# A deformable-convolution pair: the third stage's ScalarE and TensorE programs as loops, and a new order at the hand-over from the second stage

## The chip, the cores and the metric

The kernel runs on one core of one Trainium2 chip. The metric is the device time of the whole program in microseconds (us); the time before is the median of three runs.

## The reference

```python
h = _bn_lrelu(_dcnv2(x, w_off1, b_off1, w1, b1, 1, 0), g1, bb1, m1, v1)   # x: 8 x 512 x 52 x 52
h = _bn_lrelu(_dcnv2(h, w_off2, b_off2, w2, b2, 3, 1), g2, bb2, m2, v2)   # h: 256 channels in, 512 out
return x + h

def _dcnv2(x, w_off, b_off, w, b, k, pad):
    om = conv(x, w_off) + b_off            # per pixel and tap: dy, dx, mask
    oy, ox, mask = om[:, :P], om[:, P:2*P], sigmoid(om[:, 2*P:])
    val = bilinear(x, base_y + oy, base_x + ox) * mask      # P = k*k samples per pixel
    return einsum('ncphw,ocp->nohw', val, w) + b
```

`_bn_lrelu` is a batch norm followed by a leaky ReLU of slope 0.1. All arithmetic is float32.

## The kernel before

The 8 x 52 x 52 pixels are 169 tiles of 128 pixels (`TILES`), in 13 chunks of 13 tiles. Three stages follow each other, and every engine runs its part of all three in program order.

**First stage.** A 1x1 convolution: x is loaded by SP, multiplied by TensorE, and its 256 channels per pixel are written to a table in DRAM. TensorE's and ScalarE's parts are hardware loops (`Fori`) over chunks (L390, L461).

**Second stage.** One gather per tile (GpSimd, L702) fetches the four neighbours of each sampled pixel; ScalarE and VectorE weigh and add them (`near` L780, `add_far` L877, `add_upper` L893, `add_lower` L901, `activate` L910). The result h goes to a second DRAM table (`table_writes`, L302, on ScalarE's queue) and, transposed by TensorE (L715) and copied by ScalarE (L788), into a 3x3 convolution that gives the offsets of the third stage: `convolve` (TensorE, L730) per band of 8 image rows, `fold_band` (ScalarE, L802), `turn` (TensorE, L748). From the offsets a chunk's plan (weights and row indices) is made by `modulation` and `hats` (ScalarE, L815 to L832) and by `place` and `modulate` (VectorE, L926 to L945); SP writes it to DRAM (L676) and loads it again four tiles at a time (L295).

**Third stage.** 42 blocks ("supers") of 4, 3 or 2 tiles, nine taps each. A unit is one tap of one tile: a gather of 128 x 1024 floats (GpSimd, L1181) into one of 18 slots, then `scale_near` (ScalarE, L1195), `add_far` (VectorE, L1246), `scale_line` (ScalarE, L1203), `add_line` (VectorE, L1254). Four units make a tap: TensorE transposes it (L1314, 8 matmuls), ScalarE and VectorE split it into a high and a low part (`upper` L1209, `lower` L1261), and `multiply` (L1327) does 24 matmuls of 128 x 512. TensorE does the transposes of tap r and then the multiply of tap r-1. After nine taps the sums are evacuated (L1218) and finished (L1268, L1278).

**The hand-over.** The third stage's first eight units (`BEGUN`) are already scaled and added at the end of the second stage. ScalarE's loop runs on for `DRAIN = 14` steps after the last tile and does in each what of copies, folds and begun units falls due. TensorE does the first transposes in that drain, but the first multiply only after `pe.wait_ge(gate_ready, CHUNKS)`: its first matmuls would write PSUM bank 0, from which ScalarE and VectorE still read the last offsets. VectorE does the last chunk's `place` and `modulate` after the eight units, and ScalarE its `hats`, before both go on with tap 2. GpSimd's gathers are in program order; gathers 8 to 17 go to slots that the second stage still uses, first those in `h_other`, then in `h_stage` (free once the table's last writes have landed), then in the transposed h (`IN_H_T`, free after the last `convolve`) and in the offset sums (`IN_Q`, free after the last `turn`).

The helper that writes third-stage programs has two forms, both there before: `in_full` writes all taps out, `position` writes the first and last ones out and puts the middle in a loop of 19 rounds, 18 taps (two blocks) a round. Before, only `in_full` is used.

## Time and profile before

| | us |
|---|---|
| three runs | 3228.51, 3241.77, 3260.52 |
| median | 3241.77 |
| the profiled execution | 3246.28 |
| its span from the first to the last instruction | 3244.3 |
| mean granted TensorE clock | 0.984 of full speed |

The profile and all its rows are of the one profiled execution, 4.5 us above the median. 2.0 us of it lie outside the span.

### The profile page before, as it was taken

Reading aid. Unit: us, or ns where it says so; the run is one execution under the profiler, and the core shown is the slowest. Engines: PE = TensorE matmul, PEld = TensorE weight load, DVE = VectorE, ACT = ScalarE, POOL = GpSimd, SP = SyncE. Lnnn points to the kernel's source line nnn. Section 1 sums busy time; section 2 is a strip of 40 time slices with the busy share of each in tenths; the row PEclk is TensorE's granted clock in tenths of the full one; section 3 lists DMA queues with packets and bytes.
Section 4 is the critical chain, followed back from the end, with each engine's and each line's share of the span. In section 5 each row is a group of like instructions: output and inputs, shape, how many; then the busy total and the mean of one; then the engine's idle time right before and its main releaser. Section 6 shows DMA issues by size and latency. Waiting matters only on the chain.

```text
span 3244.3 us, 48817 instructions
## 1 busy us (share of the span) xinstructions
PE 3042.3 (94%) x15660; PEld 2474.0 (76%) x15660; DVE 2741.7 (85%) x4746; ACT 2498.5 (77%) x4658; POOL 1744.9 (54%) x1708
## 2 busy tenths in 40 slices
PE   8997888889999999999999999999999999999999
PEld 7996455478777778777878777778777777777879
DVE  5557999879888889888989888889888888888987
ACT  5665777778787878788888787878788778778876
POOL 0003444456666566665666666666665656665652
PEclk9998999989999999999999999999999999999999
DMA  9998999999999999998999999999999999998995
GB/s 324 366 353 318 387 347 332 321 377 355 356 361 345 364 356 347 351 369 323 372 367 353 354 370 339 370 353 343 358 357 333 360 343 330 345 360 324 356 346 188
DMA packets 431464, 1125.10 MB, mean 347 GB/s; under 512 B 42956, under 2 KB 171468, under 8 KB 431232
## 3 DMA queue, kind: packets, MB, share of 16 engines
q0 software_dynamic: 244784, 891.09, 74.2%
q1 hardware_dynamic: 118608, 163.05, 14.1%
q10 hardware_dynamic: 67840, 68.16, 6.1%
q8 instruction: 110, 1.80, 0.2%
q14 instruction: 122, 1.00, 0.1%
HBM read 1002.15 MB, written 137.04 MB: 351 GB/s over the span
## 4 chain that ended last, share of the span: by engine, by line
PE 44%; DVE 32%; ACT 12%; issue 8%; another core or an unknown queue 3%; ACTq 1%; DMA 0%; SPq 0%; DVEq 0%; POOLq 0%
PE psum_t L1327 29%; DVE arena L1246 11%; DVE val_lo L1261 6%; PE psum_t L400 5%; PE psum_t L1314 5%; ACT psum_t L1195 5%; PE psum_t L730 4%; DVE arena L1254 4%; ACT arena L1203 2%; DVE val_first L1254 2%; DVE z_sb L1268 2%; ACT val_hi L1209 2%; DVE arena L877 2%; DVE arena L1278 1%
## 5 line engine op out<-in xcount | busy, mean ns | idle before, releaser
L1181 POOL DMA_INDIRECT arena<-table,plan_in x1521 | 1571.4, 1033 | 1017.6 <-DVE arena L1254 444.4
L1327 PE MATMUL psum_t<-val_hi,w_hi 128*128 128x512 f32 (+2 forms) x3096 | 1247.2, 403 | 50.9 <-ACT z_sb L1218 30.8
L1327 PE MATMUL psum_t<-val_hi,w_lo 128*128 128x512 f32 (+2 forms) x3096 | 1205.7, 389 | 8.9 <-issue 8.7
L1327 PE MATMUL psum_t<-val_lo,w_hi 128*128 128x512 f32 (+2 forms) x3096 | 1204.0, 389 | 4.5 <-issue 4.3
L1195 ACT ACTIVATE psum_t<-arena,plan_in 128x512 f32<-128x512 f32 x1521 | 1042.4, 685 | 211.6 <-DVE arena L1246 119.9
L1246 DVE SCALAR_TENSOR_TENSOR arena<-arena,plan_in,psum_t 128x512 f32<-128x512 f32 x1521 | 1129.3, 742 | 72.4 <-issue 38.6
L1327 PEld LDWEIGHTS psum_t<-val_hi,w_hi 128*128 128x128 f32 x3096 | 587.7, 190 | 187.8 <-ACT z_sb L1218 50.4
L1261 DVE TENSOR_TENSOR val_lo<-psum_t,val_hi 128x1024 fp32r<-128x1024 f32 (+2 forms) x387 | 465.5, 1203 | 275.3 <-ACT val_hi L1209 167.5
L1327 PEld LDWEIGHTS psum_t<-val_hi,w_lo 128*128 128x128 f32 x3096 | 586.0, 189 | 132.8 <-issue 11.8
L1327 PEld LDWEIGHTS psum_t<-val_lo,w_hi 128*128 128x128 f32 x3096 | 588.9, 190 | 108.1 <-issue 5.9
L1209 ACT ACTIVATE val_hi<-psum_t 128x1024 fp32r<-128x1024 f32 (+2 forms) x387 | 386.4, 998 | 272.7 <-remote 185.5
L1203 ACT ACTIVATE arena<-arena,plan_in 128x256 f32<-128x256 f32 x1014 | 503.5, 497 | 0.1
L1254 DVE SCALAR_TENSOR_TENSOR arena<-arena,plan_in 128x256 f32<-128x256 f32 x1014 | 487.8, 481 | 0.0
L1314 PE MATMUL psum_t<-ident,arena 128*128 128x128 f32 x2028 | 271.3, 277 | 54.1 <-DVE arena L1254 45.1
L1314 PEld LDWEIGHTS psum_t<-ident,arena 128*128 128x128 f32 x2028 | 237.6, 143 | 99.1 <-DVE arena L1254 63.8
L702 POOL DMA_INDIRECT arena<-table,arena x169 | 164.2, 972 | 259.6 <-DVE arena L901 109.5
L1203 ACT ACTIVATE val_first<-arena,plan_in 128x256 f32<-128x256 f32 x507 | 253.2, 499 | 0.1
L1254 DVE SCALAR_TENSOR_TENSOR val_first<-arena,plan_in,val_first 128x256 f32<-128x256 f32 x507 | 243.3, 480 | 0.0
L730 PE MATMUL psum_t<-arena 128*96 128x408 f32 (+1 forms) x624 | 237.1, 517 | 0.0
L400 PE MATMUL psum_t<-w_hi,val_hi 128*128 128x260 f32 x676 | 197.8, 293 | 28.5 <-DVE val_lo L520 27.8
L520 DVE TENSOR_TENSOR val_lo<-arena,val_hi 128x512 fp32r<-128x512 f32 x169 | 116.3, 691 | 123.9 <-ACT val_hi L418 123.4
L400 PE MATMUL psum_t<-w_hi,val_lo 128*128 128x260 f32 x676 | 193.0, 286 | 0.0
(90 smaller groups left out, 2396.8 us busy)
## 6 DMA issues: line engine op xcount, KB each, us to landing
arena<-x SPq DMA_DIRECT2D x90, 512.0 KB, 4.7
table<-arena ACTq DMA_DIRECT2D x40, 896.0 KB, 7.3
out<-arena SPq DMA_DIRECT2D x136, 256.0 KB
table<-arena ACTq DMA_DIRECT2D x40, 768.0 KB, 7.1
arena<-x SPq DMA_DIRECT2D x70, 384.0 KB, 6.3
arena<-table,plan_in POOLq DMA_INDIRECT x1521
table<-table SPq DMA_DIRECT2D x32, 512.0 KB
arena<-w POOLq DMA_DIRECT2D x9, 512.0 KB, 6.5
```

The costliest lines, as they stand in the source:

```text
L400: last = nc.tensor.matmul(y_bank(j), a[:, X_SLOT[j], k, :], b[:, k, :], start=(k == 0 and a is x_hi and b is w1_hi), stop=(k == KT1 - 1 an ...
L702: nc.gpsimd.indirect_dma_start(gather1[:, t % SLOTS, :], None, table1[0:image_end(t) + WIDTH, :], bass.IndirectOffsetOnAxis(ap=index1[:, t ...
L730: last = nc.tensor.matmul(out_rows[:, :, to:to + w], woff_sb[:, kt, dx, :], h_rows[:, :, at:at + w], start=(nth == 0 and kt == 0), stop=(n ...
L1181: nc.gpsimd.indirect_dma_start(landing(r, i)[:, :], None, rows, bass.IndirectOffsetOnAxis(ap=row.bitcast(u32), axis=0))\
L1195: nc.scalar.activation(psum_near[:, unit(r, i) % NEARS, :], landing(r, i)[:, 0:2 * C_MID], ACT.Identity, scale=weight(r, i, 0)).then_inc(n ...
L1203: nc.scalar.activation(val(r, i), landing(r, i)[:, 0:C_MID], ACT.Identity, scale=weight(r, i, 2)).then_inc(line_scaled, 1)
L1209: nc.scalar.activation(val_hi[:, r % 2, :, 0:n], psum_val[:, :, 0:n], ACT.Identity).then_inc(hi_ready, 1)
L1246: nc.vector.scalar_tensor_tensor(out=landing(r, i)[:, 0:2 * C_MID], in0=landing(r, i)[:, 2 * C_MID:4 * C_MID], scalar=weight(r, i, 1), in1 ...
L1254: nc.vector.scalar_tensor_tensor(out=v, in0=landing(r, i)[:, C_MID:2 * C_MID], scalar=weight(r, i, 3), in1=v, op0=ALU.mult, op1=ALU.add).t ...
L1261: nc.vector.tensor_tensor(val_lo[:, r % 2, :, 0:n], psum_val[:, :, 0:n], val_hi[:, r % 2, :, 0:n].bitcast(f32), ALU.subtract)\
L1314: last = nc.tensor.transpose(psum_val[:, kt, i * P:(i + 1) * P], val(r, i)[:, kt * P:(kt + 1) * P], ident[:, :])
L1327: last = nc.tensor.matmul(psum_acc[:, oc, 0:n], a[:, w, oc * P:(oc + 1) * P], b[:, r % 2, kt, 0:n], start=(w == 0 and a is w2_hi and b is ...
```

## The change

- **Third stage.** ScalarE and TensorE use `position` (a loop of 19 rounds, its bound `ROUNDS` and its 18 taken back edges the same on both); VectorE stays written out. In the built program TensorE's loop body is 622 instructions of which 576 are matmuls, and each matmul stands for a weight load and a multiply in the trace: 1198 together. ScalarE's body is 299 instructions. Waits on semaphores in the loop compare with a register that is computed ahead of them.
- **Hand-over, TensorE.** Convolutions are done one or two steps after the pair of tiles that completes a band, turns one step earlier. The first multiply goes ahead of the wait for the offsets: it does output blocks 3, 1, 2 and only before block 0 waits. Its transposes are followed by those of taps 1 and 2.
- **Hand-over, ScalarE and VectorE.** ScalarE's drain is an explicit list. VectorE's `place` is cut in two: `place_first` (the read of PSUM) stays at the hand-over, `place_rest` goes to tap 7 of the third stage, `hats` of the last chunk to tap 8 and `modulate` to tap 9.
- **Hand-over, GpSimd.** The slots' order is `h_other`, `h_t`, the offset sums, and `h_stage` last.
- **Stores.** The second table is written by SP, not by ScalarE's queue, with the last part of the last chunk cut in two; a chunk's plan is stored after the next chunk's table.

```diff
+LATE_TILE = 10
+PLACE_REST_AT = 7
...
-        PLACE = [(TILES + n) % SLOTS for n in range(SLOTS)] + IN_H_OTHER + IN_H_STAGE + IN_H_T + IN_Q
+        PLACE = [(TILES + n) % SLOTS for n in range(SLOTS)] + IN_H_OTHER + IN_H_T + IN_Q + IN_H_STAGE
...
-            DRAIN = 14
-            PLACED = 9
+            DRAIN = 9
+            FOLDED = 6
+            PLACED = 8
...
             def on_sync(sp):
-                for c in range(CHUNKS):
+                def store_h(c):
+                    for half in range(2):
+                        for j, tiles in parts_of(c, half):
+                            sp.wait_ge(h_ready, c * CHUNK + j + tiles)
+                            table_writes(sp, table2, h_buf(c), c, (j, tiles), table2_written[c % 2][half], copies_of(c))
...
+                for c in range(CHUNKS):
+                    store_h(c)
+                    if c:
+                        store_plan(c - 1)
...
+                store_plan(CHUNKS - 1)
...
-                    if t == last_tile(BAND_COUNT - 1) + PLACED:
+                    for band, nth in CONVOLVE_AT.get(t, ()):
+                        convolve(band, nth)
+                    if t == TILES + 2:
                         begin_transpose()
-                    for nth in range(3):
-                        if t - 3 - nth in BAND_AT:
-                            convolve(BAND_AT[t - 3 - nth], nth)
...
-                pe.wait_ge(chain2, (CHUNKS - 1) * (CHAIN + 1) + 1)
-                pe.wait_ge(gate_ready, CHUNKS)
+                def offsets_read():
+                    pe.wait_ge(chain2, (CHUNKS - 1) * (CHAIN + 1) + 1)
+                    pe.wait_ge(gate_ready, CHUNKS)
+
+                begin_multiply(offsets_read)
...
+                    act.wait_ge(lines_ready, TILES - 1)
+                    begin_unit(0)
+                    fold_band(before_last, 1)
+                    copy_h_t(last_pair - 1)
+                    fold_band(before_last, 2)
+                    act.wait_ge(lines_ready, TILES)
+                    act.wait_ge(upper_added, TILES)
+                    begin_unit(1)
+                    copy_h_t(last_pair)
+                    for u in range(2, 6):
+                        begin_unit(u)
+                    for dy in range(3):
+                        fold_band(last_but_one, dy)
                     begin_upper()
+                    for dy in range(3):
+                        fold_band(last, dy)
+                    for u in range(6, BEGUN):
+                        begin_unit(u)
                     modulation(CHUNKS - 1)
-                    hats(CHUNKS - 1)
+                    return lambda: hats(CHUNKS - 1)
...
-                def step(it, r):
+                def step(it, r, late_place, late_modulate):
+                    if r == PLACE_REST_AT:
+                        late_place()
+                    if r == PLACE_REST_AT + 2:
+                        late_modulate()
...
-                return lambda: transpose(0, 0), lambda: in_full(step, after=1, first=1)
+                def begin_multiply(offsets_read):
+                    multiply(0, 0, order=(3, 1, 2, 0), first_free=offsets_read)
+                    transpose(0, 1)
+
+                return lambda: transpose(0, 0), begin_multiply, lambda: position(pe, step, after=1, first=2)
```

In ScalarE's third stage `in_full(step, after=5, first=2)` becomes `position(act, ..., after=5, first=2)`.

TensorE at the hand-over, from the last bands to the first multiply. L715, L730, L748, L1314 and L1327 are the transposes of h, `convolve`, `turn`, and the third stage's transposes and multiply. Before:

```order
L715 MATMUL psum_t<-ident,arena 128x128 x2
L730 MATMUL psum_t<-arena 96x416 x2
L748 MATMUL psum_t<-arena 128x27 x3
L730 MATMUL psum_t<-arena 96x8x51 x4
L730 MATMUL psum_t<-arena 96x416 x2
L748 MATMUL psum_t<-arena 128x27 x4
L730 MATMUL psum_t<-arena 96x8x51 x4
L748 MATMUL psum_t<-arena 128x27 x3
L1314 MATMUL psum_t<-ident,val_first 128x128 x8
L748 MATMUL psum_t<-arena 128x27 x4
L1314 MATMUL psum_t<-ident,arena 128x128 x8
L1327 MATMUL psum_t<-val_hi,w_hi 128x512
```

Now (the same five are L744, L759, L777, L1374 and L1389):

```order
L744 MATMUL psum_t<-ident,arena 128x128 x2
L759 MATMUL psum_t<-arena 96x416 x2
L759 MATMUL psum_t<-arena 96x8x51 x4
L777 MATMUL psum_t<-arena 128x27 x4
L1374 MATMUL psum_t<-ident,val_first 128x128 x8
L777 MATMUL psum_t<-arena 128x27 x7
L1389 MATMUL psum_t<-val_hi,w_hi 128x512
```

After the last pair of h only three convolution groups are left, the first third-stage transposes stand ahead of the last seven turn matmuls, and the first multiply follows those turns with no transposes between.

VectorE at the same place. L1246, L1254 and L1261 are `add_far`, `add_line` and `lower`; L926 to L935 are `place`, L945 is `modulate`. Before, from the fifth unit's `add_line` on:

```order
L1254 SCALAR_TENSOR_TENSOR arena<-arena,plan_in 128x256
L1261 TENSOR_TENSOR val_lo<-psum_t,val_hi 128x1024
L926 TENSOR_TENSOR arena<-psum_t,arena 128x252
L929 TENSOR_SCALAR arena<-arena 128x252
L930 TENSOR_SCALAR arena<-arena 128x252
L931 TENSOR_TENSOR arena<-arena 128x252
L932 SCALAR_TENSOR_TENSOR arena<-arena 128x14x9
L935 TENSOR_TENSOR plan_sb<-arena 128x14x9
L945 TENSOR_TENSOR plan_sb<-arena 128x14x9 x2
L1246 SCALAR_TENSOR_TENSOR arena<-arena,plan_in,psum_t 128x512
```

Now, from the sixth unit's `add_far` on (L1294, L1302, L1309, L989 and L963 are `add_far`, `add_line`, `lower`, `modulate` and `place_first`):

```order
L1294 SCALAR_TENSOR_TENSOR arena<-arena,plan_in,psum_t 128x512
L1302 SCALAR_TENSOR_TENSOR val_first<-arena,plan_in,val_first 128x256
L989 TENSOR_TENSOR plan_sb<-arena 128x13x9 x2
L1309 TENSOR_TENSOR val_lo<-psum_t,val_hi 128x1024
L1294 SCALAR_TENSOR_TENSOR arena<-arena,plan_in,psum_t 128x512
L1302 SCALAR_TENSOR_TENSOR arena<-arena,plan_in 128x256
L1294 SCALAR_TENSOR_TENSOR arena<-arena,plan_in,psum_t 128x512
L963 TENSOR_TENSOR arena<-psum_t,arena 128x252
L1294 SCALAR_TENSOR_TENSOR arena<-arena,plan_in,psum_t 128x512
```

`lower` of tap 0 stands after six units instead of eight, and one plan instruction is left of eight before the ninth unit's `add_far`.

## Rows read from the trace of the kernel before

**Rows 1.** The page: busy time of each engine, and the chain's shares by engine.
```profile
PE 3042.3 (94%) x15660; PEld 2474.0 (76%) x15660; DVE 2741.7 (85%) x4746; ACT 2498.5 (77%) x4658; POOL 1744.9 (54%) x1708
PE 44%; DVE 32%; ACT 12%; issue 8%; another core or an unknown queue 3%; ACTq 1%; DMA 0%; SPq 0%; DVEq 0%; POOLq 0%
```
**Rows 2.** Windows: PE, PEld, DVE, ACT, POOL busy us; PEclk, DMA share, GB/s.
```profile
626.00:640.00 14.00, 11.85 (x50) 6.83 (x48) 6.09 (x12) 10.88 (x22) 3.75 (x4) 1.00 0.82 277
640.00:654.00 14.00, 4.04 (x23) 3.94 (x24) 11.12 (x23) 11.07 (x24) 9.97 (x11) 0.58 0.78 253
...
1300.00:3200.00 1900.00, 1818.59 (x8984) 1499.14 (x8984) 1657.83 (x2764) 1518.42 (x2635) 1156.51 (x1118) 0.99 0.95 351
```
**Rows 3.** The chain in order of time, start of the third stage: start us, us, what.
```profile
684.35 0.87 PE psum_t L1314 x8
685.22 5.46 PE psum_t L1327 x24
```
**Rows 4.** Timeline, TensorE at the hand-over: start us, us, what, idle before.
```profile
641.25 1.09 PE L1314 MATMUL psum_t<-ident,val_first 128*128 128x128 f32 x8 [3.40 <-DVE val_first L1254]
...
652.56 1.94 PE L1314 MATMUL psum_t<-ident,arena 128*128 128x128 f32 x8 [8.71 <-issue]
654.15 0.78 PE L1327 MATMUL psum_t<-val_hi,w_hi 128*128 128x512 f32 x1
...
661.34 0.48 PE L1327 MATMUL psum_t<-val_hi,w_hi 128*128 128x512 f32 x1
```
**Rows 5.** Timeline, ScalarE and VectorE at the hand-over.
```profile
625.95 0.46 DVE L945 TENSOR_TENSOR plan_sb<-arena 128x117 f32<-128x117 f32 x2
...
643.44 1.23 DVE L1261 TENSOR_TENSOR val_lo<-psum_t,val_hi 128x1024 fp32r<-128x1024 f32 x1 [0.60 <-ACT val_hi L1209]
...
649.05 0.75 DVE L1246 SCALAR_TENSOR_TENSOR arena<-arena,plan_in,psum_t 128x512 f32<-128x512 f32 x1
...
650.11 0.74 DVE L1246 SCALAR_TENSOR_TENSOR arena<-arena,plan_in,psum_t 128x512 f32<-128x512 f32 x1
...
624.34 0.39 ACT L832 ACTIVATE arena<-arena 128x117 f32<-128x117 f32 x1
...
642.38 1.02 ACT L1209 ACTIVATE val_hi<-psum_t 128x1024 fp32r<-128x1024 f32 x1 [0.18 <-PE psum_t L1314]
...
648.35 0.67 ACT L1195 ACTIVATE psum_t<-arena,plan_in 128x512 f32<-128x512 f32 x1
...
649.36 0.67 ACT L1195 ACTIVATE psum_t<-arena,plan_in 128x512 f32<-128x512 f32 x1
```
**Rows 6.** Timeline, GpSimd's gathers of the third stage's units 10 and 11.
```profile
630.09 0.94 POOL L1181 DMA_INDIRECT arena<-table,plan_in  x1 [0.30 <-issue]
640.98 1.03 POOL L1181 DMA_INDIRECT arena<-table,plan_in  x1 [9.95 <-issue]
```
**Rows 7.** Waits of VectorE, 700 to 3200 us, and (last) 330 to 612 us.
```profile
DVE val_lo L1261 <- ACT val_hi L1209: 144.7, 68, 6.6
DVE val_lo L1261 <- issue: 106.3, 70, 3.5
...
DVE arena L877 <- ACT psum_t L780: 9.7, 13, 4.0
```
**Rows 8.** The first stage's loop branches, TensorE and ScalarE: duration ns min/median/max.
```profile
L390 PEldq COMPARE_BRANCH  x13: 76/208/235, 35.2 to 287.0; - x13
...
L461 ACTq COMPARE_BRANCH  x10: 40/45/58, 53.9 to 234.6; - x10
```
**Rows 9.** DMA queues that carry instructions: 36 to 290 us (first), 700 to 3200 us.
```profile
q14 instruction: 5, 0.04, 0.0%
...
q8 instruction: 94, 1.54, 0.2%
q14 instruction: 98, 0.80, 0.1%
```
**Rows 10.** DMA issues from the table's line L302: issue to landing.
```profile
DMA to landing us min/median/max: 3.9/7.1/10.3
```

More of the change, by code:

```diff
@@ L287, in copies_of, with parts_of, written_to @@
             return 2 if c < WHOLE_CHUNKS else 1
-        def written_to(b, chunks):
-            return sum(copies_of(c) * 16 for c in range(b, chunks, 2))
+        def parts_of(c, half):
+            j, n = HALVES[half]
+            if c == CHUNKS - 1 and half == 1:
+                return (j, LATE_TILE - j), (LATE_TILE, j + n - LATE_TILE)
+            return ((j, n),)
+        def written_to(b, half, chunks):
+            return sum(copies_of(c) * len(parts_of(c, half)) * 16 for c in range(b, chunks, 2))
         def load_plan(sp, s):
@@ L644, in second_stage, with complete_at @@
             BAND_AT = {last_tile(band): band for band in range(BAND_COUNT)}
+            def complete_at(band):
+                return next(t for t in range(last_tile(band), TILES) if t in PAIR_AT)
+            CONVOLVE_AT = {}
+            for band in range(BAND_COUNT):
+                for nth, after in enumerate((1, 1, 2)):
+                    CONVOLVE_AT.setdefault(complete_at(band) + after, []).append((band, nth))
             def band_pieces(band, dy):
@@ L1239, in step, with go_on @@
                             evacuate(it, ended, EVACUATE[r % TAPS][i])
-                return begin_unit, lambda: upper(0, 0), lambda: in_full(step, after=5, first=2)
+                def go_on(late_hats):
+                    position(act, lambda it, r: step(it, r, late_hats), after=5, first=2)
+                return begin_unit, lambda: upper(0, 0), go_on
             def on_vector(dve):
@@ L1316, in transpose, with multiply @@
                     last.then_inc(transposed, 1)
-                def multiply(it, r):
+                def multiply(it, r, order=range(KT1), first_free=None):
                     n, k = tiles_of(r) * P, r % TAPS
                     pe.wait_ge(lo_ready, taps_to(it, r))
-                    for oc in range(KT1):
+                    for oc in order:
+                        if oc == 0 and first_free:
+                            first_free()
                         if k == 0 and exists(it, r - 1):
```

109 lines of the change are left out of this document (56 added, 53 removed).

## The prediction

> **What bounds the kernel now.** I read the page first for the engines' shares and the chain [rows 1]. TensorE is busy for 94% of the span and the chain goes through it for 44%, through VectorE for 32%; ScalarE has 12% of it, GpSimd and the DMA queues next to nothing. The windows then say where it isn't so [rows 2]: from 1300 to 3200 us TensorE is busy for 1819 of 1900 us, and DMA moves 351 GB/s at a share of 0.95, so memory is close behind; but from 640 to 654 us TensorE is busy for 4.0 of 14 us, at a granted clock of 0.58, so over four fifths of that stretch were at 1.2 GHz. That is the hand-over. In the steady third stage a tap costs 5.5 us of multiply and 0.87 us of transposes, 6.37 us [rows 3]; the 387 taps are 2465 us of it, and nothing in this change touches that. So the change can act in two places: the hand-over, once, and whatever the loops add or save at each round.
>
> **The hand-over.** The reader is to see four moments of TensorE [rows 4]: the first transposes at 641.25 us after an idle 3.4 (the last turns follow at once), then, after 8.7 us of nothing, tap 1's transposes at 652.56, the first multiply at 654.15, and the second multiply at 661.34, from which it is in step with the other engines. What it waited for is VectorE: its last work of the second stage is at 625.95, and the ninth unit's `add_far` only at 649.05 [rows 5], 23 us for eight units, a `lower` and a plan. I rebuild the new order from 624.7 us, the end of ScalarE's last `hats` before (624.34 + 0.39) [rows 5]. A unit takes ScalarE 1.01 us (from 648.35 to 649.36) and VectorE 1.06 (649.05 to 650.11) [rows 5]; `upper` takes 1.02 and `lower` 1.23 [rows 5]. Folds, smaller than a near's 0.67, I put at 0.4, an estimate.
> - ScalarE: first near 0.6, fold, copy and fold 1.6 (the copy waits for a pair that VectorE ends near 625.2), second near 0.6, short copy 0.3, units 2 to 5 in 4.1: 631.9. VectorE follows by 0.6 and ends tap 0 at 632.5.
> - TensorE: transposes 632.5 to 633.4. ScalarE is in three folds till 633.1, then `upper` till 634.4, VectorE's `lower` till 635.7. The last folds end at 635.9, the seven turns at 637.1.
> - First multiply 637.1 to 642.6 at 5.5 us, transposes of tap 1 till 643.5, then `upper`, `lower`, tap 2's transposes (3.1 us, in which TensorE idles for 2.2): second multiply at 646.6. Block 0 of the first multiply needs `modulation` and `place_first`, near 639: it is last in the list and doesn't wait.
>
> 661.3 - 646.6 = 14.7 us. Against it: TensorE's clock was at half after it had idled [rows 2], and it will idle here around 630 to 636 too; 24 matmuls at half clock cost up to 5.5 us more, so I take half of that. **Term 1: -12 us**, between -17 and -5.
>
> The gathers must keep up. Unit 11 was issued only at 640.98, after 10.9 us without an issue [rows 6], since its slot in `h_stage` waited for the table's last write. Now unit 11 takes the slot that the last `convolve` frees, units 12 and 13 those behind the turns (637), and only unit 14 needs the table. Gathers go out every 1.25 us, and units are used every 1.0 to 1.6, so I price this at nothing; if it does bind, the gain goes with it (rival B).
>
> `place_rest`, `hats` and `modulate` of the last chunk (five, six and two short instructions, some 2 us on each of two engines) go to taps 7 to 9. VectorE idles there: before `lower` it waited 144.7 + 106.3 us in 387 taps, 0.65 us a tap [rows 7]. Spread over three taps that covers most. SP stores the last plan only then, and x's first residual block and the third block's plan queue behind it on SP; both are used four taps or 25 us later. **Term 2: +1 us**, 0 to +4.
>
> **The second stage.** Moving the table's stores from ScalarE's queue to SP and the earlier convolve, fold and turn change nothing that ends there: VectorE ends that stage and waited for ScalarE for 9.7 us in 282 [rows 7]. Behind SP's new waits stand the plan's stores and the first two plan loads, which have chunks of time; VectorE's reuse of an h buffer waits for these stores two chunks later. TensorE may now stop for `copy_h_t` a step earlier, and behind it is the next transpose; it has room. **Term 3: -2 us**, 0 to -8.
>
> **The loops.** 18 back edges on each of two engines. The nearest rows are the first stage's: a taken branch of TensorE takes 0.208 us, one of ScalarE 0.045 [rows 8]. Register work for waits is computed while the engine still has queued work. At 0.2 us an edge: **term 4: +4 us**. That is the lower bound, and it holds only if the first instructions of the body are still on the engine when it branches. The first stage shows that for short bodies: from 36 to 290 us, over twelve of TensorE's back edges, no packet came on queue 8 and five on queue 14 [rows 9], while in straight code queue 8 brought 94 packets for some 24,000 of TensorE's instructions, so about 256 each. That body is 340 instructions, more than a packet. The new one is 1198, nearly five packets; ScalarE's is 299 against a first-stage body of 88, with smaller packets (0.80 MB in 98) of half the size. No row shows bodies this long. Upper bound: a fetch at each edge, rival A.
>
> The Trainium skill ("Runtime: NRT & Kernel Launch", section on instruction fetch mechanics) speaks against this change: a taken branch to a target outside the current window of two pages must wait for the page to be fetched. The same section gives TensorE room for 2048 instructions and the others 512, by which both bodies would stay. By the first sentence the result is rival A's, by the second mine; the trace's long first-stage loop without a fetch agrees with either.
>
> **Sum.** -12 + 1 - 2 + 4 = -9 us. The profiled execution would go from 3246.3 to 3237; it stood 4.5 above the median, so the median goes from 3241.8 to **3232 us** (3232.8, rounded down).
>
> **Rivals.**
> - **A, each back edge fetches (slower).** Place: ScalarE before tap 0 of each round. Price: the shortest landing of a DMA in these rows is 3.9 us [rows 10]; less the 0.65 us that VectorE idles in a tap, 3.2 us reach TensorE; TensorE's own fetch runs at the same time and is covered in part by queued matmuls. 18 x 3.2 = 58 instead of 4: 3232 + 54 = 3286. With the median landing of 7.1, 18 x 6.4 = 116: 3344. It decides from 1.8 us an edge on (32 us, 1% over the median before, is reached at (32 + 13) / 18 = 2.5). For it: nothing shows such a body kept. Against: the 340-instruction loop spans two packets and was kept. Chance 0.27; about 0.2 of it is over 1% slower.
> - **B, the gain at the hand-over is eaten.** Gathers, half clock or a late turn leave the second multiply at 659 or so: 3232 + 12 = 3244. For it: DMA is at 0.82 and 0.78 in these windows [rows 2], and TensorE at half clock. Chance 0.15.
> - **C, more than I sum up.** If both bodies stay, the code packets of [rows 9] vanish, 0.3% of DMA time or 8 us: 3224, or 3217 with the best of term 1. Chance 0.1. Faster by over 1% needs 32 us, and I find no stretch that holds them.
> - My forecast, 3232: 0.48.
>
> A tenth of a per cent can't be told here: the three runs spread over 32 us, 1%, and 1% is what a measurement of this kernel can tell from no change. The range takes in C's 3217 with some room for the median of a few runs, 3212, and above reaches A's first price: 3212 to 3286. Left out are A's dearer half and stray runs, under 0.2. Faster by over 1%: 0.05 (C and a low median). Slower by over 1%: 0.2. Within 1%: 0.75.
>
> **What would show it.** Term 1: the second multiply within 21 us of VectorE's last second-stage instruction (before 35 us), and unit 11's gather by 635. Term 2: no gap of VectorE over 2 us at taps 7 to 9 and none at the first residual. Term 4 against A: idle time of ScalarE and TensorE once in 18 taps, at the branch's line, and packets on queues 8 and 14; in my case almost no instruction packets from 700 to 3100 us on queue 8. The forecast is wrong if fetches at the edges cost more than 2.5 us each, or if the plan's late store starves the gathers of the third block.

## The result, and the profile after

The kernel after takes 3285.8 us, the median of 4 runs (3278.87 to 3295.32), against 3247.1 us of the kernel before beside it (4 runs, 3228.51 to 3260.52): ratio 1.0128, 95% interval 1.0106 to 1.015. It is slower by 1.3%, where 3232 and "no difference" had been forecast; 3285.8 lies just inside the forecast range, whose top was the price of rival A. Its profiled execution took 3295.3 us (span 3293.4), 9.5 above its median; that of before 3246.3. So 49.1 us lie between the two spans, and 38.7 between the medians.

The page after, the engines' busy time and the chain by engine; they answer to [rows 1]:

```profile
span 3293.4 us, 49916 instructions
## 1 busy us (share of the span) xinstructions
PE 3063.6 (93%) x15660; PEld 2485.3 (75%) x15660; DVE 2741.9 (83%) x4746; ACT 2493.1 (76%) x4658; POOL 1745.1 (53%) x1708
...
## 4 chain that ended last, share of the span: by engine, by line
DVE 40%; PE 26%; issue 14%; ACT 13%; another core or an unknown queue 5%; ACTq 1%; DMA 1%; SPq 0%; DVEq 0%; POOL 0%; POOLq 0%
```

TensorE's share of the chain fell from 44% to 26% and VectorE's rose from 32% to 40%. TensorE waits more; who makes it wait is the question. Windows after, the same as in [rows 2] (us; busy time of PE, PEld, DVE, ACT, POOL; granted clock, DMA share, GB/s):

```profile
626.00:640.00 14.00, 13.13 (x57) 7.24 (x55) 12.08 (x28) 11.82 (x25) 7.20 (x8) 1.00 0.99 357
640.00:654.00 14.00, 11.46 (x54) 8.26 (x53) 10.37 (x19) 12.97 (x27) 5.62 (x7) 0.88 0.80 289
1300.00:3200.00 1900.00, 1800.27 (x8809) 1478.37 (x8807) 1632.88 (x2721) 1490.63 (x2592) 1140.97 (x1101) 0.98 0.94 345
```

The hand-over looks as meant: from 640 to 654 us TensorE is busy for 11.5 us in place of 4.0. The steady third stage is worse: 1800.3 us of 1900 in place of 1818.6. Packets of instructions from 700 to 3200 us, and the branches of the loop (L1086; duration ns min/median/max), which answer to [rows 9] and [rows 8]:

```profile
q14 instruction: 60, 0.49, 0.1%
q8 instruction: 10, 0.16, 0.0%
...
L1086 ACTq COMPARE_BRANCH  x19: 40/45/50, 892.6 to 3126.9; - x19
...
L1086 PEldq COMPARE_BRANCH  x19: 83/215/217, 909.0 to 3139.4; - x19
```

TensorE's queue 8 brings 10 packets where it brought 94, ScalarE's sequencer goes on 0.2 us after each branch, TensorE's 0.06: both bodies stay on their engines. Rival A's fetch doesn't happen. VectorE's last instruction of the second stage and TensorE at the hand-over, which answer to [rows 4, 5]:

```profile
637.64 0.43 DVE L948 SCALAR_TENSOR_TENSOR arena<-arena 128x256 f32<-128x256 f32 x1
...
645.65 1.07 PE L1374 MATMUL psum_t<-ident,val_first 128*128 128x128 f32 x8
646.56 0.75 PE L777 MATMUL psum_t<-arena 97*128 97x27 f32 x6
649.38 1.07 PE L777 MATMUL psum_t<-arena 97*128 97x27 f32 x8 [2.07 <-ACT arena L833]
650.30 0.47 PE L1389 MATMUL psum_t<-val_hi,w_hi 128*128 128x512 f32 x1
...
657.47 1.03 PE L1374 MATMUL psum_t<-ident,arena 128*128 128x128 f32 x8
668.88 1.97 PE L1374 MATMUL psum_t<-ident,arena 128*128 128x128 f32 x8 [10.37 <-issue]
670.50 0.78 PE L1389 MATMUL psum_t<-val_hi,w_hi 128*128 128x512 f32 x1
```

The first transposes stand 8.0 us behind VectorE's last instruction of the second stage (15.3 before) and the first multiply 12.7 (28.2 before). But that last instruction (the first row) is itself at 637.64 us, not at 625.95 [rows 5]: **the second stage ends 11.7 us later** (from the last `activate` of the one, at 625.61, to that of the other it is 12.0). And tap 2's transposes, then, come only after 10.4 idle us.

All runs below are read by four stretches of their one profiled execution, from the starts of VectorE's `add_upper` (one per tile) and of TensorE's transposes (a tap's first weight load) in each timeline: tiles 13 to 156 of the second stage; tile 156 to the third stage's first transposes; those to tap 18's; and the 342 taps from there to tap 360, 19 rounds. (387 taps of nine a block are 43 blocks: 41 of four tiles, one of three, one of two.)

### The profile page after: what moved, and what is told of

The parts are those of the page before. It is cut to its first block, busy times and chain, and to the rows that moved or that the text cites. A ratio compares the mean times of both kernels' runs of the same rounds, so it can differ in the third digit from the quotient of the medians.

```text
span 3293.4 us, 49916 instructions
## 1 busy us (share of the span) xinstructions
PE 3063.6 (93%) x15660; PEld 2485.3 (75%) x15660; DVE 2741.9 (83%) x4746; ACT 2493.1 (76%) x4658; POOL 1745.1 (53%) x1708
## 4 chain that ended last, share of the span: by engine, by line
DVE 40%; PE 26%; issue 14%; ACT 13%; another core or an unknown queue 5%; ACTq 1%; DMA 1%; SPq 0%; DVEq 0%; POOL 0%; POOLq 0%
DVE arena L1294 16%; PE psum_t L1389 15%; DVE val_lo L1309 8%; DVE arena L1302 6%; PE psum_t L408 5%; PE psum_t L759 3%; ACT psum_t L1238 3%; DVE val_first L1302 3%; ACT arena L1246 3%; PE psum_t L1374 3%; DVE z_sb L1316 3%; DVE arena L1326 2%; ACT val_hi L1252 1%; ACT psum_t L811 1%
## 5 line engine op out<-in xcount | busy, mean ns | idle before, releaser
L1389 PE MATMUL psum_t<-val_hi,w_hi 128*128 128x512 f32 (+2 forms) x3096 | 1251.4, 404 | 44.0 <-issue 24.2
L1389 PE MATMUL psum_t<-val_lo,w_hi 128*128 128x512 f32 (+2 forms) x3096 | 1210.1, 391 | 5.8 <-issue 5.5
L1389 PE MATMUL psum_t<-val_hi,w_lo 128*128 128x512 f32 (+2 forms) x3096 | 1209.1, 391 | 5.5 <-issue 5.3
L1294 DVE SCALAR_TENSOR_TENSOR arena<-arena,plan_in,psum_t 128x512 f32<-128x512 f32 x1521 | 1124.5, 739 | 52.4 <-ACT psum_t L1238 37.8
L1309 DVE TENSOR_TENSOR val_lo<-psum_t,val_hi 128x1024 fp32r<-128x1024 f32 (+2 forms) x387 | 464.5, 1200 | 334.3 <-ACT val_hi L1252 180.9
L1389 PEld LDWEIGHTS psum_t<-val_hi,w_hi 128*128 128x128 f32 x3096 | 591.0, 191 | 176.7 <-issue 38.8
L1389 PEld LDWEIGHTS psum_t<-val_hi,w_lo 128*128 128x128 f32 x3096 | 589.6, 190 | 131.2 <-issue 9.0
L1389 PEld LDWEIGHTS psum_t<-val_lo,w_hi 128*128 128x128 f32 x3096 | 591.5, 191 | 111.9 <-issue 8.8
L1246 ACT ACTIVATE arena<-arena,plan_in 128x256 f32<-128x256 f32 x1014 | 503.1, 496 | 0.0
L1302 DVE SCALAR_TENSOR_TENSOR arena<-arena,plan_in 128x256 f32<-128x256 f32 x1014 | 484.3, 478 | 0.0
L1374 PE MATMUL psum_t<-ident,arena 128*128 128x128 f32 x2028 | 273.6, 279 | 84.0 <-DVE arena L1302 73.3
L1374 PEld LDWEIGHTS psum_t<-ident,arena 128*128 128x128 f32 x2028 | 237.9, 143 | 131.8 <-issue 99.8
L759 PE MATMUL psum_t<-arena 128*96 128x408 f32 (+1 forms) x624 | 243.3, 528 | 39.5 <-ACT arena L819 25.4
L1246 ACT ACTIVATE val_first<-arena,plan_in 128x256 f32<-128x256 f32 x507 | 253.0, 499 | 0.0
L1302 DVE SCALAR_TENSOR_TENSOR val_first<-arena,plan_in,val_first 128x256 f32<-128x256 f32 x507 | 242.1, 477 | 0.0
L759 PEld LDWEIGHTS psum_t<-arena 128*96 128x96 f32 x624 | 97.5, 167 | 136.3 <-issue 80.9
```

What stands on the lines that cost most here:

```text
L759: last = nc.tensor.matmul(out_rows[:, :, to:to + w], woff_sb[:, kt, dx, :], h_rows[:, :, at:at + w], start=(nth == 0 and kt == 0), stop=(n ...
L1246: nc.scalar.activation(val(r, i), landing(r, i)[:, 0:C_MID], ACT.Identity, scale=weight(r, i, 2)).then_inc(line_scaled, 1)
L1294: nc.vector.scalar_tensor_tensor(out=landing(r, i)[:, 0:2 * C_MID], in0=landing(r, i)[:, 2 * C_MID:4 * C_MID], scalar=weight(r, i, 1), in1 ...
L1302: nc.vector.scalar_tensor_tensor(out=v, in0=landing(r, i)[:, C_MID:2 * C_MID], scalar=weight(r, i, 3), in1=v, op0=ALU.mult, op1=ALU.add).t ...
L1309: nc.vector.tensor_tensor(val_lo[:, r % 2, :, 0:n], psum_val[:, :, 0:n], val_hi[:, r % 2, :, 0:n].bitcast(f32), ALU.subtract)\
L1374: last = nc.tensor.transpose(psum_val[:, kt, i * P:(i + 1) * P], val(r, i)[:, kt * P:(kt + 1) * P], ident[:, :])
```

## The experiments

Each run's ratio is to executions of the kernel before beside it, on the same chip. The runs stand in five groups, and the kernel before alone takes two clearly different times in them: 3227.3, 3253.6 and 3249.0 us in runs 1 to 4, 9 to 12, 17 and 18 (the slow chip; the result's 3247.1 is of this kind), and 3075.3 and 3074.8 us in runs 5 to 8 and 13 to 16 (the quick chip). The two names are short for these times; whether it is the chip that differs isn't shown: the record gives the number 0 to the chip of runs 5 to 8, quick, and to that of runs 9 to 12, slow. What the traces show to differ is in the last section. `Old drain` means that the hand-over and the plan steps are those of the kernel before, too; `new` has the new ones.

| run | loops | second stage | chip | ratio (95%) | tiles 13-156 | to transposes | taps 0-18 | 19 rounds |
|---|---|---|---|---|---|---|---|---|
| before | none | old | slow | 1 | 288.2 | 40.6 | 131.9 | 2323.9 |
| after | both | new | slow | 1.0128 (1.0106-1.0150) | 297.5 | 33.6 | 141.5 | 2356.2 |
| e9, after again | both | new | slow | 1.0130 (1.0104-1.0156) | 297.3 | 33.7 | 143.1 | 2360.5 |
| e1 | none | new | slow | 1.0050 (1.0033-1.0068) | 297.9 | 33.6 | 139.9 | 2301.1 |
| e12 | TensorE | new | slow | 1.0064 (1.0042-1.0086) | 297.8 | 33.6 | 140.9 | 2337.9 |
| e17 | ScalarE | new | slow | 1.0040 (1.0017-1.0062) | 297.1 | 33.6 | 140.2 | 2322.2 |
| e3 | both | old, old drain | slow | 1.0093 (1.0073-1.0113) | 284.7 | 40.6 | 135.7 | 2327.3 |
| e10, as e3 | both | old, old drain | slow | 1.0077 (1.0057-1.0097) | 291.4 | 40.5 | 134.9 | 2356.4 |
| e4 | none | convolutions new, rest old, old drain | slow | 1.0165 (1.0146-1.0183) | 333.6 | 43.1 | 132.8 | 2307.1 |
| e2 | both | convolutions old, rest new | slow | 1.0446 (1.0425-1.0466) | 390.7 | 41.1 | 137.8 | 2340.7 |
| e11 | none | old, new drain | slow | 1.0002 (0.9985-1.0020) | 286.0 | 37.7 | 140.5 | 2327.8 |
| e18 | none | old, new drain | slow | 0.9990 (0.9969-1.0011) | 282.4 | 35.5 | 141.1 | 2323.6 |
| e14, after again | both | new | quick | 1.0004 (0.9995-1.0013) | 293.8 | 33.6 | 121.0 | 2170.6 |
| e16, as e1 | none | new | quick | 1.0005 (0.9996-1.0014) | 294.3 | 33.6 | 121.6 | 2170.6 |
| e5 | TensorE | new | quick | 1.0003 (0.9994-1.0012) | 292.0 | 33.6 | 120.5 | 2170.6 |
| e6, e13 | ScalarE | new | quick | 1.0001, 1.0000 (both ±0.0009) | 293.8, 292.2 | 33.7, 33.6 | 120.8, 120.7 | 2170.6 |
| e15, as e3 | both | old, old drain | quick | 1.0001 (0.9992-1.0010) | 285.9 | 40.5 | 120.6 | 2170.6 |
| e8 | both, shifted | old, old drain | quick | 1.0047 (1.0034-1.0061) | 286.3 | 40.5 | 120.5 | 2184.7 |
| e7, as e11 | none | old, new drain | quick | 0.9975 (0.9966-0.9985) | 282.5 | 36.0 | 120.6 | 2170.6 |

**First group: loops and second stage, each undone and each alone.** e1 writes both third stages out:

```diff
-                    position(act, lambda it, r: step(it, r, late_hats), after=5, first=2)
+                    in_full(lambda it, r: step(it, r, late_hats), after=5, first=2)
...
-                return lambda: transpose(0, 0), begin_multiply, lambda: position(pe, step, after=1, first=2)
+                return lambda: transpose(0, 0), begin_multiply, lambda: in_full(step, after=1, first=2)
```

> The changed kernel with the loops of the third stage on ScalarE and TensorE undone: both engines are written out in full again, everything else as after. Theory L (the loops cost about 1.5 us a round beyond what their branches take, seen as 122.3 against 124.0 us for a round of 18 taps): about 27 us less than the kernel after, 3259 us, and tap times at the last two taps of a round back at 6.7 and 6.3 us. Rival R (the loops cost nothing, the rounds run longer because of what the hand-over or the plan steps left behind): 3284 to 3286 us. Both expect VectorE to end the second stage at 638 us as in the kernel after.

3241.4 us, ratio 1.0050. The kernel before took 3227.3 beside it, so the ratios are to be compared: from 1.0128 and 1.0130 it is 0.0079 less, 26 us, as theory L said (27). The two kernels did not run beside each other, and each ratio is known to about 0.002. VectorE still ends the second stage as late as in the kernel after. e3 is the other way round, the kernel before with `in_full` changed to `position` for ScalarE and TensorE:

> The kernel before with nothing changed but the third stage of ScalarE and TensorE as loops over pairs of blocks. Theory L: 3247 + 27 = 3274 us. Rival R: 3247 to 3251 us (18 back edges at about 0.2 us).

1.0093, and 1.0077 when repeated (e10): 30 and 25 us, each beside the kernel before. The pairs agree: on the slow chip both loops cost 25 to 30 us, 1.4 to 1.7 us for each of 18 back edges, and rival R is out. e2 and e4 were to do the same for the convolutions' places, e2 with this line in the kernel after, e4 with the new table of places in the kernel before:

```diff
-                    CONVOLVE_AT.setdefault(complete_at(band) + after, []).append((band, nth))
+                    at = complete_at(band) + after if band >= BAND_COUNT - 4 else last_tile(band) + 3 + nth
+                    CONVOLVE_AT.setdefault(at, []).append((band, nth))
```

> The changed kernel with the convolutions of all but the last four bands back at their old places on TensorE, one step (4 matmuls) in each of the tiles last+3, +4 and +5, in place of two steps at the tile right after the last transposes and one behind them. Folds, turns, stores on SP, loops as after. Theory S (the early convolutions wait for ScalarE's copies with the next transposes queued behind them, so the copy of the next pair and the near scaling behind it come late, about 1 us a chunk): VectorE ends the second stage near 627 us in place of 638, and the whole takes 10 to 12 us less, 3275 us. Rival Q (the second stage is slower because SP issues its stores, or because the folds and the tail come a tile earlier): second stage still ends at 636 to 638, 3284 to 3286 us.

> The kernel before with nothing changed but the places of the convolutions on TensorE: those of the kernel after, with folds one tile later than there and turns where they were. Theory S: second stage of VectorE ends near 637 us in place of 626, whole 3257 to 3259 us. Rival Q: 3247 us.

Both theories missed: 1.0446 (3375.4 us) and 1.0165 (3279.9). Moving the convolutions without the folds breaks the step between the two engines. Waits of e2 from 345 to 600 us (us in total, times, longest; L834 is the fold, L760 the convolution, L745 the transposes of h, L812 `near`, L916 `add_far`):

```profile
ACT arena L834 <- PE psum_t L760: 106.3, 29, 6.5
...
PE psum_t L745 <- DVE arena L949: 59.6, 28, 3.7
...
DVE arena L916 <- ACT psum_t L812: 68.4, 25, 5.2
```

ScalarE stands in front of each fold until TensorE has convolved, `near` stands behind the fold, and VectorE behind `near`. The engines stand in a ring: VectorE ends a pair of tiles, TensorE transposes and convolves it, ScalarE copies, folds and scales the next tile, and VectorE goes on with that. These two runs show how dear a broken step in that ring is, not what the change costs in it; for that, all places had to go back together.

**Second group, on the quick chip.** e5 undoes ScalarE's loop alone, e6 TensorE's (one of the two lines above each). e7 undoes both and puts convolutions, folds, turns and the tail's copy of all but the last chunk back where the kernel before has them:

```diff
+                    at = complete_at(band) + after if band >= BAND_COUNT - 4 else last_tile(band) + 3 + nth
...
+                        if t == last_tile(band) + (8 if band >= BAND_COUNT - 4 else 9):
+                            turn(band)
...
+                                if t == last_tile(band) + (6 if band >= BAND_COUNT - 4 else 7) + dy:
+                                    fold_band(band, dy)
...
-                            if j == 8:
+                            if j == (9 if c < CHUNKS - 1 else 8):
                                 keep_tail(c - 1)
```

> The changed kernel with ScalarE's third stage written out again and TensorE's left as a loop. The loops together cost 29 us (the kernel before with both loops took 1.0093 of before). Theory A (ScalarE's loop is what makes the last-but-one tap of a round late, since ScalarE is at its back edge about 3 us ahead of that tap's transposes): this run is within 5 us of the changed kernel with both written out, a ratio of 1.005. Theory T (TensorE's loop costs it): a ratio of 1.013 to 1.014, as the changed kernel.

> The changed kernel with TensorE's third stage written out again and ScalarE's left as a loop. Theory A: ratio 1.013 to 1.014. Theory T: 1.005. If each engine's loop costs a part, the two runs add up: their ratios less 1.005 sum to about 0.009.

> The changed kernel with both loops undone and with convolutions, folds, turns and the tail's copy of all but the last chunk at the places of the kernel before (convolve at last+3, +4, +5, fold at +7 to +9, turn at +9, tail at tile 9), so that only the stores on SP, the drain of the last chunk and the moved plan steps are new. Theory S (the early convolutions and folds as a whole cost the second stage 11 us): VectorE ends the second stage at 626 to 628 us in place of 638, the ratio falls from 1.005 to 1.000 to 1.002. Rival Q (the stores on SP cost it): the second stage still ends at 636 to 638 us, ratio 1.005. If the new drain gains what was forecast, 12 us, and nothing takes it back, 0.996 to 0.998.

e5 and e6 came out the same, 1.0003 and 1.0001, and say nothing of A and T, since here no version's loops could be told from none (e14 and e15 below). e7 is the one that matters: 3067.3 us, 0.9975, 8.0 us under the kernel before, and by the ratios 9 us under e16, which differs from it only in the old places. VectorE's tiles 13 to 156 take 282.5 us in place of 294.3. So **theory S in its wide form holds**: the new places of convolve, fold, turn and tail cost it, not the stores on SP (rival Q), which e7 keeps. How is seen in the waits from 345 to 600 us, of e16 (new places; L759 convolution, L819 copy of h, L833 fold, L811 `near`, L915 `add_far`):

```profile
PE psum_t L759 <- ACT arena L819: 20.0, 20, 1.6
PE psum_t L759 <- ACT arena L833: 10.4, 10, 1.3
...
ACT arena L819 <- issue: 53.3, 29, 2.9
ACT arena L819 <- PE psum_t L744: 5.9, 10, 1.8
...
DVE arena L915 <- ACT psum_t L811: 11.7, 17, 1.0
```

and of e7 (old places; L745 transposes of h, L760 convolution, L835 fold, L821 copy, L813 `near`, L918 `add_far`):

```profile
PE psum_t L745 <- DVE arena L951: 28.1, 20, 3.3
...
ACT arena L835 <- PE psum_t L760: 36.4, 40, 1.7
ACT arena L821 <- issue: 14.7, 29, 1.3
...
DVE arena L918 <- ACT psum_t L813: 3.2, 10, 1.1
```

With the old places TensorE waits for VectorE alone, for new tiles. With the new ones it stands in front of a convolution until ScalarE has copied the pair (20 times, 20.0 us) or folded (10.4), and the next pair's transposes stand behind the convolution. ScalarE then waits for those transposes in front of its next copy, 53.3 us in place of 14.7, the next `near` stands behind the copy, and VectorE waits 11.7 us in place of 3.2. (The profile calls most of this wait `issue`; that it is one for the transposes is read from `copy_h_t`, which waits for their mark, and from the 5.9 us that are put down to L744.) In all ScalarE idles here little more than with the old places, 59 us against 51; of those 51, 36.4 stand in front of the folds, now all stand in front of the copies. So the rows show where the idle time moved to and that VectorE's grew; the links between are read from the program. Which of the moved places does it was not separated; e2 and e4 show that they can't be moved one by one.

e8 starts a loop's body four taps later, in the kernel before with both loops:

```diff
-                for r in range(first, ROUND_TAPS):
+                for r in range(first, ROUND_TAPS + 4):
...
-                    for r in range(ROUND_TAPS):
+                    for r in range(4, ROUND_TAPS + 4):
```

> The kernel before with both loops of the third stage, but with a loop's body starting four taps later (tap 4 of a pair of blocks, where no wait of TensorE was seen), so that the back edges fall elsewhere in the ring of waits; the same 18 or 19 back edges. Theory edge (each back edge costs about 1.5 us wherever it stands): 1.009. Theory place (it costs because it falls on the taps where the block changes and TensorE's transposes are late anyway): 1.002 or less.

1.0047, and e15 without the shift 1.0001: 14 us, 0.8 at each back edge. But neither theory is right. After the shift ScalarE's sequencer stands still for 5.1 us behind every taken branch (5.04 to 5.23, once 4.88) where it stood 0.2. Packets of instructions from 900 to 3000 us, e8 and then e15, and ScalarE behind the branch at 1226.60 of e8:

```profile
q14 instruction: 136, 1.11, 0.1%
...
q14 instruction: 51, 0.42, 0.1%
...
1229.86 0.52 ACT L1203 ACTIVATE val_first<-arena,plan_in 128x256 f32<-128x256 f32 x1
1231.96 0.69 ACT L1195 ACTIVATE psum_t<-arena,plan_in 128x512 f32<-128x512 f32 x1 [1.58 <-DVE arena L1246]
```

85 more packets, 4.7 for each of the 18 back edges. ScalarE has 3.7 us of work queued and then idles 1.6 us in front of `near`. This is rival A after all, in another kernel: a body of 301 instructions that begins elsewhere in the code is fetched at each round, one of 299 was not. The edit changed both the body's length and its start, and no run separates them.

**Third group, on the slow chip again.**

> The changed kernel itself, unchanged, beside the three below on one chip; runs 5 to 8 came from a chip on which the kernel before takes 3075 us and the third stage's rounds take 114.2 us with TensorE never idle, runs 1 to 4 from one with 3227 us and rounds of 121 to 124 us. If this is the quick chip: theory C (a back edge costs only when both engines have one, since the shifted pair of loops cost 14 us there and a single loop nothing) gives 1.003 to 1.005; theory N (unshifted loops are free where TensorE never waits) gives 1.000. If the slow chip: 1.013 again.

> The kernel before with both loops. Quick chip: theory C 1.003 to 1.005, with the taps after a back edge at 6.5 to 6.7 us in place of 6.33; theory N 1.000. Slow chip: 1.009 again.

> The changed kernel without loops and with the old places of convolutions, folds, turns and tail for all but the last chunk. Quick chip: 0.9975 again. Slow chip: theory S says that the 11 us of the second stage come back there too (the ratio of both loops undone was 1.005), 1.001 or less, with VectorE ending the second stage near 626 us.

> The changed kernel with only TensorE's loop kept. Quick chip: 1.0003 again. Slow chip: theory A (ScalarE's back edge is the one that delays) 1.005; theory T (TensorE's) 1.013; both in part, between.

e9 and e10 repeat 1.013 and 1.008. e11, 1.0002, repeats theory S on the slow chip: 0.0048 less than e1's ratio, 16 us, of which 11.9 are in tiles 13 to 156. e12, 1.0064, excludes theory T, TensorE's loop as the whole cost.

**Fourth group, on the quick chip.**

> The changed kernel with only ScalarE's loop kept. Slow chip: if ScalarE's loop carries the 27 us, 1.012 to 1.013; if the cost needs both, 1.005 to 1.007. Quick chip: 1.000 again.

> The changed kernel itself. Slow chip 1.013 again. Quick chip: 1.000 if loops are free there (one loop alone gave 1.000), 1.003 to 1.005 if two loops cost what the shifted pair cost.

> The kernel before with both loops, not shifted. The trace of the shifted pair showed ScalarE's sequencer standing 5.1 us behind every back edge where the unshifted ones stand 0.2 us, so on the quick chip 1.000 to 1.001 is expected here and 1.0047 was the price of those 5.1 us. Slow chip 1.008 again.

> The changed kernel with both loops undone. Quick chip: the same as with one loop, 1.000, which makes the new order of the second stage worth plus 8 us there against the run with the old order (0.9975). Slow chip: 1.005 again.

All four lie within 0.05% of the kernel before. Here the change as a whole does nothing, and the loops cost nothing: 19 rounds take 2170.6 us in every kernel but e8, 6.35 us a tap. Windows of the kernel after from 1300 to 3000 us, slow chip, then quick chip:

```profile
1300.00:3000.00 1700.00, 1605.20 (x7851) 1317.22 (x7850) 1457.55 (x2428) 1330.75 (x2315) 1016.29 (x981) 0.98 0.94 345
...
1300.00:3000.00 1700.00, 1700.00 (x8575) 1429.24 (x8574) 1587.58 (x2644) 1452.27 (x2526) 1114.35 (x1071) 1.00 0.99 375
```

**Fifth group, slow chip.** e17 is e6 again. e18 is e11 with the switch to the new places one band later and the tail's copy at its old place in the last chunk too, since VectorE had taken 28.1 us (e7: 26.3) for its last twelve tiles, where the kernel after took 24.2 and that before 23.4.

> The changed kernel with only ScalarE's loop kept. Slow chip: if ScalarE's loop carries the 27 us, 1.012 to 1.013; if the cost needs both engines' loops, 1.005 to 1.007. Quick chip: 1.000 for the third time.

> The changed kernel with both loops undone, and with the old places of convolutions, folds and turns kept up to the last chunk's first band (the earlier run switched one band sooner, and VectorE then took 26.3 us for the last twelve tiles in place of 23.4 to 24.2), the tail's copy at its old place throughout. New: the drain, the stores on SP, the moved plan steps. If the switch is smoother now, 2 to 3 us below the earlier run: 0.9965 on the quick chip, 0.999 on the slow one. If the pile-up only moves, 0.9975 and 1.000.

e17, 1.0040, excludes theory A too. Neither loop alone can be told from none (1.0064 and 1.0040 against 1.0050, each known to about 0.002), together they cost 0.0079: on this chip it takes both, or nearly so (ratios from three groups of runs are compared here). e18 is at 0.9990 on the slow chip, within its interval of 1 and of e11; the last twelve tiles took 25.7 us. The best shown version is e7, 0.25% under the kernel before on the quick chip and, as e11, even with it on the slow one.

## Why the prediction was wrong, step by step

**Term 1, hand-over, -12 (-17 to -5).** The mechanism was right. Behind VectorE's last second-stage instruction the first transposes were forecast at 6.5 us and came at 8.0, the first multiply at 11.2 and came at 12.7 (before 15.3 and 28.2). The second multiply was forecast at 20.7 us; on the quick chip it came at 26.5 and in the result at 32.9, before 35.4. TensorE and ScalarE there, e14, VectorE's last instruction at 634.11:

```profile
646.76 0.47 PE L1389 MATMUL psum_t<-val_hi,w_hi 128*128 128x512 f32 x1
...
653.93 1.03 PE L1374 MATMUL psum_t<-ident,arena 128*128 128x128 f32 x8
659.02 1.97 PE L1374 MATMUL psum_t<-ident,arena 128*128 128x128 f32 x8 [4.05 <-DVE arena L1302]
660.64 0.77 PE L1389 MATMUL psum_t<-val_hi,w_hi 128*128 128x512 f32 x1
...
654.63 0.69 ACT L1238 ACTIVATE psum_t<-arena,plan_in 128x512 f32<-128x512 f32 x1 [1.35 <-DMA arena<-table,plan_in]
```

Of the missing 5.8 us, 1.5 are the late start, 1.7 the first multiply, which runs at 1.2 GHz in part, 1.9 the wait for tap 2, of which 1.35 is ScalarE's wait for a gather (the gathers, of which the prediction said "I price this at nothing"), and 0.75 tap 2's transposes at half clock. The second multiply began at half clock too. Unit 11's gather kept its forecast (8.2 us behind VectorE's last instruction in the kernel after, forecast 9), but unit 12's then waited 4.5 us for the last turns and went out 13.6 us behind it, where 11 had been assumed. At tap 18 the gain measured from tile 156 is 161.1 - 154.6 = 6.5 us on the quick chip: half the term, inside its range. On the slow chip the first transposes gain the same 7.0, and at tap 18 nothing is left: taps 0 to 18 take 137.8 to 143.1 us with the new drain against 131.9 to 135.7 with the old one (121 against 120.6 on the quick chip). Of the 9.6 us between the kernels after and before, 3.8 lie in the step from tap 1's transposes to tap 2's (11.6 us for 7.8), where TensorE idles for the 10.4 us of the row at 668.88 above, and 3.4 in that from tap 9's to tap 10's (term 2). At the first of them ScalarE's split of tap 1 came 7 us behind the end of its transposes (657.47 + 1.03):

```profile
665.49 1.02 ACT L1252 ACTIVATE val_hi<-psum_t 128x1024 fp32r<-128x1024 f32 x1 [6.32 <-remote]
```

That is rival B's outcome, though its reasons, half clock and gathers, explain only what the quick chip shows; on the slow one it is late splits of the kind described in the last section, whose cause is open.

**Term 2, moved plan steps, +1.** On the quick chip taps 9 to 18 take 57.1 us, nine times 6.35, so nothing was lost there. On the slow one the step from tap 9's transposes to tap 10's takes 8.8 to 9.8 us in all eight runs with the moved steps, and 6.2 to 7.6 in the four without (before, e3, e4, e10); VectorE waits there up to 6.0 us behind ScalarE's `val_hi`. Some 2 to 3 us more than forecast may so belong to this term, but the same runs also have the new drain, and none has one without the other: it stays open.

**Term 3, second stage, -2: this step failed first.** Its sentence "TensorE may now stop for `copy_h_t` a step earlier, and behind it is the next transpose; it has room" named the mechanism and took the room for granted. TensorE's waits for VectorE with the old places (28.1 us in e7's rows) were no room for a wait in front of the transposes: they came at the wrong point of the ring, where the next copy and the next `near` depend on it. Measured: tiles 13 to 156 took 297.5 us for 288.2 (+9.3), on the quick chip 293.8 for 285.9 (+7.9). The rest of the term was right: with the old places and SP's stores they take 282.5 (e7) for 285.9 and 286.3 (e15, e8) on the quick chip, -3.4; on the slow one, where equal second stages differ by up to 6.7 (e3, e10), 286.0 and 282.4 for 284.7 to 291.4.

**Term 4, loops, +4 and no fetch.** Right that both bodies stay, right in size on the quick chip (0 measured), wrong by 22 us on the slow chip, of whose kind the result is: 26 us. What failed is the step from "the branch takes 0.2 us" to "so TensorE loses 0.2 us". The branches take just that; the rounds are longer at the last taps of a round. TensorE's step from tap 16 to tap 17 takes 7.1 us on average before and 8.2 after, and that from 17 to the next 0 takes 6.3 and 6.8. Over the five slow traces with both loops and the four with none (before, e1, e4, e11) a round takes 1.75 us more with them: 1.0 at that first step, 0.3 at the second and 0.4 from tap 7 to tap 8. What makes the taps late stays open.

**The sums.** Quick chip: +7.9 in tiles 13 to 156, -6.5 from tile 156 to tap 18, +0 in the rounds: +1.4, measured +0.0004, 1.2 us; the forecast "no difference" holds there. e7: -3.4 - 4.5 = -7.9, measured -8.0. Slow chip, spans: +2.0 up to tile 13, +9.3, -7.0 to the first transposes, +9.6 in taps 0 to 18, +32.3 in 19 rounds and +3.1 behind them, 49.3 for the 49.1 between the spans; the rounds of single executions of one kernel differ by up to 29 us (e3 against e10). By the ratios the loops are 26 of the 42 us (0.013) and the rest, 16, is the second stage. Against the forecast of -9 that makes three misses: term 4 by 22 us, term 3 by about 11 (+9.3 for -2), and term 1, which comes to nothing there, by 12; together 45 of the 51 us between -9 and +42; the 6 left are less than single traces differ by. Rival A's price, 3286, is the measured time, but by other means: no edge fetched, and that the range reached so far up was luck.

## What to carry to other kernels

When an in-order engine gets an instruction earlier, ask not how idle that engine is but what it then stands in front of: here the early convolutions waited for ScalarE, and the transposes behind them fed ScalarE's next copy and so VectorE's next tile. Producer and consumer of a ring (convolve and fold) have to be moved together or not at all; moved alone they cost 53 us (e4) and some 100 (e2 less the kernel after), where the joint move costs 9 (e16 less e7) to 16 (e1 less e11). A loop that isn't fetched is not yet free, and a loop that fits may stop fitting when its body starts elsewhere or grows a little (e8 did both): look at the packets of instructions and at the sequencer's step behind the branch, not at the length alone.

## What the runs showed of the hardware

**Two speeds of one kernel.** The same kernel before takes 3075 us in some groups of runs ("quick chip") and 3227 to 3254 in others ("slow chip"); the mean granted clock of all kernels is 0.991 to 0.996 in the first and 0.968 to 0.989 in the second. Whether two kinds of chips are behind it or something else that changes with time or place, no run shows. Stages 1 and 2 are alike to 1% (tiles 13 to 156: 285.9 and 288.2 us); the third is not, 6.35 us a tap against 6.7 to 6.9. On the quick chip TensorE never idles there (1700.00 of 1700 us, above). On the slow one ScalarE waits at some taps for the mark of a transpose long after the trace has it ended. Waits of ScalarE from 1300 to 3000 us in the kernel after, slow chip, then quick chip (`remote` is a releaser that the trace doesn't place):

```profile
ACT val_hi L1252 <- remote: 164.8, 40, 6.9
...
ACT val_hi L1252 <- PE psum_t L1374: 95.5, 91, 2.2
```

One such place, tap 16 of a round (tap 88 of all), in the kernel after (TensorE, then ScalarE), and the same tap of e1 without loops:

```profile
1266.81 1.03 PE L1374 MATMUL psum_t<-ident,arena 128*128 128x128 f32 x8
1267.60 0.48 PE L1389 MATMUL psum_t<-val_hi,w_hi 128*128 128x512 f32 x1
...
1267.03 0.49 ACT L1246 ACTIVATE arena<-arena,plan_in 128x256 f32<-128x256 f32 x1
1271.26 1.03 ACT L1252 ACTIVATE val_hi<-psum_t 128x1024 fp32r<-128x1024 f32 x1 [3.74 <-remote]
```

```profile
1255.95 1.03 PE L1374 MATMUL psum_t<-ident,arena 128*128 128x128 f32 x8
1256.74 0.48 PE L1389 MATMUL psum_t<-val_hi,w_hi 128*128 128x512 f32 x1
...
1256.24 0.49 ACT L1246 ACTIVATE arena<-arena,plan_in 128x256 f32<-128x256 f32 x1
1258.95 1.03 ACT L1252 ACTIVATE val_hi<-psum_t 128x1024 fp32r<-128x1024 f32 x1 [2.22 <-remote]
```

By the trace the transposes end at 1267.84 and 1256.98, and ScalarE's split of that tap starts 3.4 and 2.0 us later, with nothing queued ahead of it. (Ends of matmuls are modelled, so whether the mark is late or TensorE is, the trace can't say.) From a tap's last weight load to ScalarE's start it is 0.4 us at tap 16 of the median round on the quick chip (e14), 1.7 to 3.1 on the slow one without loops (before, e1, e4, e11), 3.7 to 4.5 with both (after, e2, e9, e3, e10), 3.7 with TensorE's alone (e12). The same is seen at taps 1, 7 and 10 of a round, in kernels with and without loops (in the fifth group at 8 and 17 in place of 7 and 16). And at every 24th tap (25, 49 and so on to 337, some 164 us apart) TensorE's matmuls stand 0.6 to 5 us apart for some 2 to 9 us, mostly with a stretch at 1.2 GHz behind them. The quick chip has none of this. The loops' cost sits at taps 16, 17 and 7. Why the marks come late there, and why two loops lengthen it, stays open: no run took the cause away. One lead is untested: these taps return with each block of nine, as SP's loads of x do, and in the slow traces before the fifth group a late tap 7 or 16 stands some 5 us behind such a load in 28 to 34 of 38 blocks (6 to 12 in the fifth). The quick chip issues the same loads at the same taps and has no late mark, so they can't be the whole cause.

**A loop's place in the code.** In e8 ScalarE's sequencer stood still for 5.1 us behind each branch. The Trainium skill ("Runtime: NRT & Kernel Launch", section on instruction fetch mechanics) states that a taken branch to a target outside the engine's window must wait for a fetch; e8's rows agree, with 5.1 us and 4.7 packets an edge. It also puts that window at two pages; here the measurements differ, since TensorE's body of 1198 instructions, nearly five of its packets of 16 KB, came back 18 times without one (no packet on queue 8 from 909 to 3139 us of the kernel after).
